# Expert results of a routed layer: added to rows of X in DRAM by the scatter itself, in place of a stored list, a reload and sums

## The reference

```python
x = x + 0.5 * moe(layernorm(x))

def moe(x):                      # E = 8 experts, K = 2 of them for each token
    xn = x * rsqrt(mean(x * x) + eps) * ln_w
    vals, idx = top_k(xn @ Wg + bg, 2)
    we = sum(one_hot(idx, 8) * softmax(vals)[..., None], axis=-2)
    for e in range(8):           # F = 512 hidden features
        y = (silu(xn @ W1a[e] + b1a[e]) * (xn @ W1b[e] + b1b[e])) @ W2[e] + b2[e]
        out = out + we[:, e] * y
    return out
```

## Time and profile before

| | us |
|---|---|
| median of the runs | 776.2 |
| time of the profiled execution | 776.33 |
| its span in the trace | 774.5 |
| TensorE (PE) busy | 625.8 (81%) |
| VectorE (DVE) busy | 451.8 (58%) |
| ScalarE (ACT) busy | 430.7 (56%) |
| GpSimd (POOL) busy | 310.3 (40%) |
| granted TensorE clock, mean share | 0.906 |

### The profile page before, as it was taken

How to read it: one execution, slowest core, us unless ns; L and a number is a source line. 1 busy time by engine, 2 the same in 40 slices (tenths; PEclk the granted TensorE clock), 3 DMA queues, 4 the chain that set the end, 5 groups by cost and what they waited for, 6 DMA issues and landing times.

```text
span 774.5 us, 13285 instructions
## 1 busy us (share of the span) xinstructions
PE 625.8 (81%) x4674; PEld 464.5 (60%) x4674; DVE 451.8 (58%) x1417; ACT 430.7 (56%) x816; POOL 310.3 (40%) x388
## 2 busy tenths in 40 slices
PE   6889886469999997079887699999569669999990
PEld 4667683222222223077687589999557668999990
DVE  6872959831123115983958455556469774555572
ACT  5664634579999997454635544344343554443450
POOL 1143353213232321234432467766240036776543
PEclk9689999559999999589998799999869869999995
DMA  8311000668100000011003676667310058666655
GB/s 321 121 45 68 1 2 0 195 212 306 53 2 1 1 2 1 0 52 61 2 2 63 208 262 185 223 184 220 112 57 1 2 144 275 223 187 222 178 162 169
DMA packets 36468, 87.59 MB, mean 113 GB/s; under 512 B 5168, under 2 KB 20144, under 8 KB 35376
## 3 DMA queue, kind: packets, MB, share of 16 engines
q1 hardware_dynamic: 31280, 76.13, 29.9%
q0 software_dynamic: 5120, 10.58, 4.9%
HBM read 69.75 MB, written 16.94 MB: 112 GB/s over the span
## 4 chain that ended last, share of the span: by engine, by line
PE 49%; ACT 17%; DVE 16%; issue 8%; DMA 5%; POOL 3%; SPq 0%; ACTq 0%; DVEq 0%; POOLq 0%
PE ps L2020 17%; ACT arena L1493 9%; PE ps L2032 9%; PE ps L1724 3%; PE ps L1820 2%; PE ps L1933 2%; ACT Xn L1301 2%; DMA arena<-xs,wqk 2%; PE ps L1766 1%; DMA arena<-in_wq 1%; PE ps L1775 1%; PE ps L1799 1%; PE ps L1910 1%; DVE stats L666 1%; DMA arena<-yd 1%
## 5 line engine op out<-in xcount | busy, mean ns | idle before, releaser
L2020 PE MATMUL ps<-arena 128*128 128x256 f32 (+1 forms) x768 | 151.6, 347 | 2.9 <-issue 1.3
L1546 ACT ACTIVATE arena<-ps,arena 128x256 f32<-128x256 f32 (+1 forms) x192 | 84.1, 439 | 124.5 <-issue 76.1
L2020 PEld LDWEIGHTS ps<-arena 128*128 128x128 f32 x768 | 125.8, 191 | 18.3 <-DVE arena L1017 3.5
L1493 ACT ACTIVATE arena<-ps 128x1024 f32<-128x1024 f32 x144 | 132.5, 1320 | 2.5 <-PE ps L1910 2.2
L1017 DVE SCALAR_TENSOR_TENSOR arena<-ps,arena 128x256 f32<-128x256 f32 (+1 forms) x192 | 84.2, 440 | 76.0 <-ACT arena L1546 73.9
L639 POOL DMA_INDIRECT yd<-arena,wqk x80 | 78.7, 983 | 61.2 <-DVE arena L1039 49.0
L603 POOL DMA_INDIRECT arena<-xs,wqk x80 | 77.6, 970 | 38.1 <-issue 15.2
L590 POOL TENSOR_SCALAR_AFFINE_SELECT arena<-arena 128x512 f32<-128x512 f32 x64 | 39.9, 636 | 106.6 <-ACT arena L1493 106.6
L1933 PE MATMUL ps<-arena 128*32 128x512 f32 (+3 forms) x768 | 79.7, 503 | 1.0
L2032 PE MATMUL ps<-arena 128*128 128x128 f32 x640 | 79.4, 275 | 0.0
L2032 PEld LDWEIGHTS ps<-arena 128*128 128x128 f32 x640 | 75.2, 192 | 0.4
(11 more groups left out here) (297 smaller groups left out, 1151.4 us busy)
## 6 DMA issues: line engine op xcount, KB each, us to landing
arena<-in_wall SPq DMA_DIRECT2D x48, 836.0 KB, 4.7
arena<-slots SPq DMA_DIRECT2D x2, 2048.0 KB, 7.8
arena<-scr_q SPq DMA_DIRECT2D x8, 512.0 KB, 6.7
arena<-scr_k SPq DMA_DIRECT2D x8, 512.0 KB, 7.6
arena<-yd SPq DMA_DIRECT2D x8, 512.0 KB, 5.6
xs<-Xn SPq DMA_DIRECT2D x8, 260.0 KB, 5.3
scr_q<-arena SPq DMA_DIRECT2D x4, 384.0 KB, 4.5
scr_k<-arena SPq DMA_DIRECT2D x4, 384.0 KB, 4.1
```

The costliest lines, as they stand in the source:

```text
L1493: nc.scalar.activation(Pa[:, n0:n0 + FILL, :], ps[:, bank:bank + FILL, :], ACT.Exp, scale=AD ** -0.5).then_inc(sem("exp", i), 1)
L1546: nc.scalar.activation(sl[:, k % 3, 0:rows], ps[:, k % 3, 0:rows], ACT.Silu, bias=raw[:, slot, EW_BA + f:EW_BA + f + 1]).then_inc(sem("sil ...
L2020: ins = mm(ps[:, bank, 0:rows], raw[:, slot, w + P * f:w + P * (f + 1)], xTt[:, j % 2, 0:rows], start=True, stop=True)
```

## The change

The picks' results are no longer stored one row per pick. At the start of an expert layer SP stores X itself to a DRAM tensor of rows (`summed_rows`: an internal tensor `x_rows` in the first expert layer, the output tensor in the second). The scatter of a column then adds its rows to that tensor (`compute_op=ALU.add`); `dest` is the token, or a spare row behind the tokens. A transfer that adds reads a row and writes it later, and two tiles may hold the two picks of one token, so POOL now waits before each tile's scatter until the scatter of the tile before has landed; before the first it waits for the stored X. The two columns of a wide tile belong to one expert, so they never hold the same token, and are issued together.

After the last scatter the first expert layer reloads X, four chunks of 256 KB, and VectorE takes the row statistics; POOL's sums, VectorE's sums and their signals are gone. In the second expert layer nothing is reloaded and nothing is stored: the program ends when the last scatter has landed. The output tensor has spare rows at its end, which the host cuts off.

```diff
 # x_of
-            return (sem("x_chunk"), NC * (i - 1) + c + 1) if i else (sem(f"chunk_in{c}"), 16)
+            if i == 0 or kinds[i - 1] == "moe":
+                return sem(f"chunk_in{c}"), 16 * (1 + kinds[:i].count("moe"))
+            return sem("x_chunk"), NC * (sum(kind != "moe" for kind in kinds[:i]) - 1) + c + 1
...
-        yd = nc.dram_tensor("yd", (2 * ROWS + COLS * P, D), F32, kind="Internal").ap()
+        summed_rows = [nc.dram_tensor("x_rows", (ROWS + COLS * P, D), F32, kind="Internal").ap(), out]
...
 # SP, start of an expert layer
+                x_rows = summed_rows[before]
+                for c in range(NC):
+                    sp.wait_ge(*x_of(i, c))
+                    sp.dma_start(x_rows[HALF * c:HALF * (c + 1), :].rearrange("(t p) d -> p t d", p=P), X[:, 4 * c:4 * c + 4, :]
+                                 ).then_inc(sem("stored_x", i), 16)
                 sp.wait_ge(*at("expgap", i, 2))
...
 # SP, end of an expert layer, when all y_out have landed
-                for c in range(NC):
-                    sp.dma_start(yf[:, 4 * c:4 * c + 4].rearrange("p t k d -> p t (k d)"),
-                                 yd[HALF * 2 * c:HALF * 2 * (c + 1), :].rearrange("(t p k) d -> p t (k d)", p=P, k=2)
-                                 ).then_inc(sem(f"chunk_in{c}"), 16)
+                if i < last:
+                    for c in range(NC):
+                        sp.dma_start(X[:, 4 * c:4 * c + 4, :], x_rows[HALF * c:HALF * (c + 1), :].rearrange("(t p) d -> p t d", p=P)
+                                     ).then_inc(sem(f"chunk_in{c}"), 16)
...
-            for c in range(NC):
-                sp.wait_ge(*x_of(last + 1, c))
-                sp.dma_start(out[:, 4 * c:4 * c + 4, :], X[:, 4 * c:4 * c + 4, :]).then_inc(sem("stored"), 16)
-            sp.wait_ge(sem("stored"), 16 * NC)
...
 # POOL, the scatter of tile j
                     pool.wait_ge(*at("y", i, j + 1))
+                    if j:
+                        n = before * NTILE + j - 1
+                        pool.wait_ge(sem(f"y_out{n % YSLOT}"), landed(n, YSLOT))
+                    else:
+                        pool.wait_ge(*at("stored_x", i, 16 * NC))
                     col, width = TILES[j]
                     for h in range(width):
                         nc.gpsimd.indirect_dma_start(
-                            out=yd, out_offset=bass.IndirectOffsetOnAxis(ap=dest[:, col + h:col + h + 1], axis=0),
-                            in_=y_[:, slot, h, :], in_offset=None).then_inc(sem(f"y_out{slot}"), 16)
-                for c in range(NC):
-                    ts = slice(4 * c, 4 * c + 4)
-                    pool.wait_ge(sem(f"chunk_in{c}"), 16 * (before + 2))
-                    nc.gpsimd.tensor_tensor(yf[:, ts, 0, :], yf[:, ts, 0, :], yf[:, ts, 1, :], ALU.add
-                                            ).then_inc(sem("ysum", i), 1)
+                            out=summed_rows[before], out_offset=bass.IndirectOffsetOnAxis(ap=dest[:, col + h:col + h + 1], axis=0),
+                            in_=y_[:, slot, h, :], in_offset=None, compute_op=ALU.add).then_inc(sem(f"y_out{slot}"), 16)
...
 # VectorE, the index list: token instead of 2 x token + pick
-                nc.vector.scalar_tensor_tensor(out=free, in0=total, scalar=0.0, in1=route[:, RC_SPARE:RC_SPARE + COLS],
-                                               op0=ALU.is_equal, op1=ALU.mult)
-                link(nc.vector.scalar_tensor_tensor(out=dst_, in0=total, scalar=2.0, in1=second, op0=ALU.mult, op1=ALU.add))
-                nc.vector.scalar_tensor_tensor(out=dest, in0=dst_, scalar=-2.0, in1=free, op0=ALU.add, op1=ALU.max
+                link(nc.vector.scalar_tensor_tensor(out=free, in0=total, scalar=0.0, in1=route[:, RC_SPARE:RC_SPARE + COLS],
+                                                    op0=ALU.is_equal, op1=ALU.mult))
+                nc.vector.scalar_tensor_tensor(out=dest, in0=total, scalar=-1.0, in1=free, op0=ALU.add, op1=ALU.max
                                                ).then_inc(sem("index", i), 1)
...
 # VectorE, end of an expert layer
-                for c in range(NC):
-                    dve.wait_ge(*at("ysum", i, c + 1))
-                    x_chunk = X[:, 4 * c:4 * c + 4, :]
-                    nc.vector.tensor_tensor(x_chunk, x_chunk, yf[:, 4 * c:4 * c + 4, 0, :], ALU.add).then_inc(sem("x_chunk"), 1)
-                    dve.wait_ge(*x_of(i + 1, c))
-                    if i < last:
+                if i < last:
+                    for c in range(NC):
+                        dve.wait_ge(*x_of(i + 1, c))
                         row_stats(c, i + 1)
...
-    out = nc.dram_tensor("out_x", (P, NT, D), F32, kind="ExternalOutput").ap()
+    out = nc.dram_tensor("out_x", (ROWS + COLS * P, D), F32, kind="ExternalOutput").ap()
```

More of the change, by code:

```diff
@@ L126 @@
                 stored_rows=16 * NC, xtp=NTILE, xt=NTILE, up=NTILE * FT, silu=NTILE * FT, h=NTILE * FT,
-                down=NTILE, sum=NTILE, y=NTILE, ysum=NC),
+                down=NTILE, sum=NTILE, y=NTILE, stored_x=16 * NC),
 }
@@ L300, in build @@
         v |= carve([("raw", WSLOT * EW), ("xt", XSLOT * HT * ROW), ("xT", 2 * TS),
-                    ("sl", 3 * TS), ("hT", 2 * FT * TS), ("y", YSLOT * HT * D), ("apart", 4096), ("yf", NT * 2 * D)])
+                    ("sl", 3 * TS), ("hT", 2 * FT * TS), ("y", YSLOT * HT * D), ("apart", 4096)])
         lg, eq_, re_ = (v[k].rearrange("p (t e) -> p t e", t=NT) for k in ("lg", "eq", "re"))
@@ L314, in build @@
         tab = v["tab"].bitcast(mybir.dt.int32)
-        total, second, dst_, free = (v[k] for k in ("sum", "second", "dst", "free"))
+        total, second, free = (v[k] for k in ("sum", "second", "free"))
         wt = v["wt"].rearrange("p (k h) -> p k h", k=3)
@@ L327, in build @@
         y_ = v["y"].rearrange("p (i h d) -> p i h d", i=YSLOT, h=HT)
-        yf = v["yf"].rearrange("p (t k d) -> p t k d", t=NT, k=2)
         xs = nc.dram_tensor("xs", (ROWS, ROW), F32, kind="Internal").ap()
-        yd = nc.dram_tensor("yd", (2 * ROWS + COLS * P, D), F32, kind="Internal").ap()
+        summed_rows = [nc.dram_tensor("x_rows", (ROWS + COLS * P, D), F32, kind="Internal").ap(), out]
+        assert kinds[-1] == "moe" and kinds.count("moe") == 2
         v = carve([("lqT", B * T), ("lK", NT * D), ("lV", NT * (D + 1)), ("lE", B * T), ("loc", B * T),
@@ L2160, in _layout @@
     route[:, RC_COL:RC_COL + COLS] = np.arange(COLS)
-    route[:, RC_SPARE:RC_SPARE + COLS] = 2 * ROWS + P * np.arange(COLS) + p
+    route[:, RC_SPARE:RC_SPARE + COLS] = ROWS + P * np.arange(COLS) + p
     route[:, RC_TOK:RC_TOK + PICKS] = P * (np.arange(PICKS) % NT) + p + 1
@@ L2235 @@
     r = run_bass_kernel_spmd(nc, [in_map], core_ids=[0])
-    return r.results[0]["out_x"].transpose(1, 0, 2).reshape(B, T, D)
+    return r.results[0]["out_x"][:ROWS].reshape(B, T, D)
```

## The result

The changed kernel takes 839.47 us (median of 4 runs, 838.14 to 840.83), the kernel before 776.1 on the same chip: 1.082 times as long, interval 1.0789 to 1.0852. The prediction was 772.5 and faster; the kernel is 63 us slower, outside the range. The profiled executions took 839.72 and 776.33.

What follows compares the result with a forecast made beforehand. TensorE, half the chain, was taken as the bound. From 776.3 us: last layer -13.7 + 3.5 + 7d, middle -5.5 + 3.5 + 7d, together -12.2 + 14d; with d = 0.6, -3.8, or 772.5; range 764.5 to 783.5.

Steps and rivals of the forecast that it cites:

- The ends: After each layer's last scatter: shorter reload, sums and store gain 13.7 us in the last layer, 5.5 in the middle.
- the wide tiles: Wide tiles of both expert layers: each scatter moves by about 0.3 us plus d without piling up, counted as nothing.
- this wait of VectorE: Expert layers: VectorE waits for a scatter's landing three tiles on, when it needs the y buffer again; no size given.
- POOL's spare 0.33: Wide tiles: POOL's four indirect transfers fill 5.12 of 5.45 us, leaving 0.33 per tile, so delay does not pile up.
- POOL becomes the bound: Rival, chance 0.09: adding scatters taking over 1.15 us to issue outgrow the wide tile's 5.45; at 1.48, 783.5 us.
- The bare chain: Wide tiles without cover: a step from scatter to scatter of 1.30 + 2.24 + 0.28 + d us, still under 5.45.
- d: Extra time of an adding transfer over a plain one: taken as 0.6 us, between 0 and 1.4; break-even at 0.87.
- The break at d = 1.6: Wide tiles: the uncovered scatter-to-scatter step stays under 5.45 us until d passes 1.6.
- The tail: Last seven narrow tiles of each layer: scatters follow landing by landing, 2.52 us a step plus d, costing 3.5 + 7d.
- The slow adding: Rival, chance 0.22: same chain of landings with d over 0.87, decided in narrow tiles; at 1.2, +4.6, 780.9 us.
- The middle: Rival, chance 0.09: between the layers the reload's first chunk lands no earlier, some 2 of 5.5 us go: 774.5.
- Queues that take turns: Rival, chance 0.08: scatters take turns with weight loads, tile 17 lands in time, the chain keeps up: 762.0 us.

## Why the prediction was wrong

- **The ends** were right in mechanism and size: -12.9 and -5.0, forecast -13.7 and -5.5. The store of X cost nothing that shows.
- **The step that failed is the wide tiles**, "For the wide tiles I count nothing", with its reason "issued 1 us later behind the same weight load it lands no later, and POOL has 0.33 to spare per tile". They cost 28.0 and 30.1: 58 of the 67 by which the forecast of -3.8 missed the 63. Three causes, shown by what went when each was taken away:
  - The load is not the same load. A landing now releases both the next scatter and, through the y buffer and VectorE, the next weight load. The prediction had this wait of VectorE in its list and did not follow it to SP. Small loads take away 12.6 and 14.4 per layer. The link is only a part of that: with eight buffers 4.6 and 6.2 went, and loads still stood ahead of scatters.
  - POOL's spare 0.33 had to take two issues that are 0.63 longer each (1.61). This was the trigger of the rival "POOL becomes the bound", given 0.09; its price was per tile right in kind (6.43, where it worked out 5.45 + 0.67 = 6.12), and too small because it knew only that cause. Beyond the loads it is 6.0 and 6.5 per layer (the step from small loads to no gathers as well); in the add alone, with no wait, it was 10.
  - The bare chain was set at 1.30 + 2.24 + 0.28 + d, under 5.45. All its terms were short: 1.85 to the second issue, 3.3 for the landing, 0.74 for the wake. At 5.9 it is over 5.45 on its own, 9 per layer. The break at d = 1.6 was reckoned with the issue of before, though d was the very thing in doubt.
- **The tail** was right in mechanism and short in size. Narrow steps and last landing cost 12.2 and 10.9 a layer, forecast 3.5 + 7 x 0.6 = 7.7. Issue to landing is 3.2 to 3.3, so d is 1.0 (0.6 of it in the issue), inside its bounds, and the wake 0.73 instead of 0.28: that figure was read where POOL waited for one semaphore, and here it waits for two. Without the add this term alone makes the step 2.99 instead of 2.52.
- **The rivals.** The slow adding had d right (over 0.87) and the sum (at 1.2, 780.9) far off, for it too took the wide tiles at nothing. The middle did gain. Queues that take turns were to make the kernel faster, and it is slower; whether they take turns is another matter, below.

The Trainium skill, DMA: Bandwidth & Descriptors, section Queues, rings and completion order, has the queues served in turn, packet by packet. The trace shows both: against it, no packet of POOL's queue beside 112 of a load up to 508.6; with it, 66 beside 81 in 515.0 to 516.5, and in the run with eight y buffers 122 beside 102 in 499 to 501. What the loads cost the wide tiles either way is bounded by the 12.6 and 14.4 per layer that the small loads gave back.

By the Trainium skill, Collectives: The Full Stack, section The bandwidth ceiling, a reducing transfer reads two sources per chunk. The prediction priced the second read at 0.2 by the earlier trace rows. Measured, d is 1.0. Of that 0.6 lies in the issue, and the trace shows where to look for the rest: an adding transfer takes 0.83 us of each engine (23.6% of 16 engines over 3.5 us, row below), the plain one 0.20.

Of the prediction's own signs of being wrong, two came: a scatter's issue grew, and the wide tiles stretched. The third, last scatters that wait for VectorE, did not.

**What stays open.** The chain's parts were taken away on top of one another (loads, then gathers), so their shares depend on that order; only the whole is fixed. Why an adding scatter issues slower was not tried, and why a load's packets go alone in one step and beside POOL's in the next is not shown.

## What to carry to other kernels

A wait for the landing of the transfer before turns a pipelined stretch into a chain: price one full circle (wake, issue, landing) against the stretch's own step before anything is called hidden, with the new instruction's price in every term. Then follow what the landing releases beside the waiting instruction: here it was a large load that started with the scatter and ran ahead of it. And an engine with 0.33 to spare in 5.45 is not a cover for an instruction of unknown length.

## What the runs showed of the hardware

- An adding scatter of 128 rows of 512 B holds POOL for 1.55 to 1.74 us where the plain one takes 0.98, and lands 3.2 to 3.3 from its start instead of 2.24. It moves 144 packets for 128 rows and takes 0.83 us of each engine, against 32 packets and 0.20 for a plain one. The software queue around one of them (584.4 to 587.9):

```profile
q0 software_dynamic: 144, 0.07, 23.6%
```

- Of two waits ahead of a POOL transfer, the order decides the wake: 0.73 from the landing where the landing is waited for last, 0.25 where it is waited for first and the other semaphore is already there. In this kernel that is 15 to 16 us.
- Transfers on POOL's queue can wait out most of a load on SP's (no packet while 112 of the load's 144 moved), and can also move beside one, nearly packet for packet (66 beside 81 in 515.0 to 516.5).
- TensorE's granted clock fell where it had less work: it was busy 43.35 of 58 us in 497 to 555, at a mean clock of 0.97; then, while narrow tiles kept it busy 19.78 of 42, the mean was 0.71, between its two levels, 1.2 and 2.4 GHz (columns: busy PE, PEld, DVE, ACT, POOL; clock, DMA share, GB/s). There the chain of landings set the pace, so it cost nothing that the chain shows.

```profile
497.00:555.00 58.00, 43.35 (x272) 38.28 (x270) 21.89 (x73) 17.83 (x43) 36.99 (x28) 0.97 0.62 152
555.00:597.00 42.00, 19.78 (x120) 18.69 (x120) 11.80 (x51) 8.87 (x23) 20.25 (x14) 0.71 0.31 43
```
